# Order of the last stage: the turning of the second half's normed rows behind the first four experts of half 0, its gate behind the next four

## The reference

```python
scores = sigmoid(x @ gate.T)                      # 8 experts
sel    = top 2 of the better group of 4 (by scores + corr_bias)
top    = scores[sel] / (scores[sel].sum() + 1e-20)
lat    = x @ fc1.T                                # 256 -> 128
comb   = sum over sel of top[e] * relu2(lat @ w1[e].T) @ w2[e].T
out    = layernorm(x + comb @ fc2.T + relu2(x @ up.T) @ down.T)   # relu2(a) = max(a, 0)**2
```

## Time and profile before

| | |
|---|---|
| median of 3 runs | 1975.12 us (1972.39 to 1977.35) |
| the profiled execution's own time | 1973.6 us |
| its span, first to last instruction | 1971.5 us |
| TensorE busy | 94% of the span |
| VectorE, ScalarE, GpSimd busy | 69%, 44%, 44% |
| mean granted TensorE clock | 0.981 of full speed |

### The profile page before, as it was taken

One profiled execution on the slowest core, in us unless ns is written; L12 is line 12 of the kernel. 1 busy time (PEld: TensorE's weight loads), 2 busy tenths in 40 slices (PEclk: granted clock), 3 DMA queues, 4 the chain that ended last, 5 costly groups with the idle time before them and its releaser, 6 DMA issues.

```text
span 1971.5 us, 35531 instructions
## 1 busy us (share of the span) xinstructions
PE 1859.1 (94%) x11760; PEld 1623.9 (82%) x11760; DVE 1353.2 (69%) x3192; ACT 871.9 (44%) x1623; POOL 865.5 (44%) x1169
## 2 busy tenths in 40 slices
PE   7999999399999989999999999999999999999996
PEld 6888887289999977888788888878878878878885
DVE  5688888644444556786786886876876786786664
ACT  4445454333333424445445445445355445444443
POOL 4267777631111142454354354364265265255054
PEclk9999999599999989999999999999999999999998
DMA  4111222223332231211111221121112212111011
GB/s 155 65 65 64 75 96 87 87 75 99 107 103 86 96 106 44 66 44 60 64 51 47 50 79 44 44 87 44 44 67 65 43 47 85 38 49 54 12 44 65
DMA packets 81639, 133.04 MB, mean 67 GB/s; under 512 B 11328, under 2 KB 62144, under 8 KB 81376
## 3 DMA queue, kind: packets, MB, share of 16 engines
q1 hardware_dynamic: 71984, 104.96, 15.7%
q0 software_dynamic: 9520, 26.36, 5.5%
HBM read 105.57 MB, written 25.72 MB: 67 GB/s over the span
## 4 chain that ended last, share of the span: by engine, by line
PE 61%; DVE 7%; issue 5%; POOL 3%; ACT 3%; DMA 1%; POOLq 0%; DVEq 0%; ACTq 0%
PE c_ps L118 10%; PE c_ps L120 9%; PE c_ps L119 9%; PE b_ps L118 5%; PE b_ps L119 5%; PE b_ps L120 5%; PE c_ps L133 3%; PE c_ps L134 3%; PE c_ps L135 3%; PE c_ps L2023 2%; PE c_ps L2084 2%; PE c_ps L2086 2%; PE c_ps L2085 2%; POOL c_pool_tmp L97 1%; ACT b_win_raw L1610 1%
## 5 line engine op out<-in xcount | busy, mean ns | idle before, releaser
L1547 POOL TENSOR_TENSOR c_place<-c_shared_place,c_place 128x512 fp32r<-128x512 f32 x256 | 324.5, 1296 | 197.2 <-ACT c_place L1726 114.1
L1538 POOL DMA_INDIRECT c_gathered<-expert_results,c_slots x112 | 112.3, 1003 | 325.2 <-DVE c_pre L1778 301.7
L1937 DVE SCALAR_TENSOR_TENSOR c_shared_place<-c_ps,c_shared_place 128x512 f32<-128x512 f32 x256 | 170.4, 683 | 57.3 <-ACT c_shared_place L1718 57.1
L118 PE MATMUL c_ps<-c_place 128*128 128x256 f32 (+1 forms) x520 | 149.9, 288 | 10.4 <-DVE c_place L1850 6.4
L1726 ACT ACTIVATE c_place<-c_shared_place 128x512 fp32r<-128x512 f32 x128 | 80.3, 630 | 173.6 <-DVE c_shared_place L1937 172.6
L133 PE MATMUL c_ps<-c_downT_hi,c_place 128*128 128x256 f32 x512 | 151.4, 296 | 2.7 <-POOL c_place L1547 2.7
L119 PE MATMUL c_ps<-c_place 128*128 128x256 f32 (+1 forms) x520 | 147.9, 284 | 0.0
L120 PE MATMUL c_ps<-c_place 128*128 128x256 f32 (+1 forms) x520 | 147.8, 284 | 0.0
L134 PE MATMUL c_ps<-c_downT_lo,c_place 128*128 128x256 f32 x512 | 144.7, 283 | 0.0
L135 PE MATMUL c_ps<-c_downT_hi,c_place 128*128 128x256 f32 x512 | 144.6, 282 | 0.0
L1047 POOL DMA_INDIRECT b_xs<-x_rows,expert_tokens x56 | 57.9, 1033 | 196.5 <-PE b_ps L1228 176.4
(11 more groups left out here) (416 smaller groups left out, 6144.6 us busy)
## 6 DMA issues: line engine op xcount, KB each, us to landing
c_x2T<-score_rows SPq DMA_DIRECT2D x64, 512.0 KB, 5.5
b_win_raw<-xT SPq DMA_DIRECT2D x8, 1024.0 KB, 6.4
a_x_rows<-x SPq DMA_DIRECT2D x8, 1024.0 KB, 5.6
x_rows<-a_x SPq DMA_DIRECT2D x8, 1024.0 KB, 4.5
c_pre<-x_rows SPq DMA_DIRECT2D x8, 1024.0 KB, 5.5
out<-b_win_raw SPq DMA_DIRECT2D x16, 512.0 KB, 3.0
b_win_raw<-w_in SPq DMA_DIRECT2D x7, 1024.0 KB, 5.5
b_wout_raw<-w_out SPq DMA_DIRECT2D x7, 1024.0 KB, 6.3
```

The source lines that it names most:

```text
L118: pe.matmul(out, lh, rh, start=(j == 0), stop=False)
L1538: pool.indirect_dma_start(rows[:, a, :], None, d["ys"], bass.IndirectOffsetOnAxis(ap=slots[:, a, t:t + 1], axis=0), bounds_check=TRASH + P ...
L1547: pool.tensor_tensor(hid_lo[:, place, :], square[:, place % RING, :], f32(hid_hi[:, place, :]), ALU.subtract).then_inc(hid_split, 1)
L1937: v.scalar_tensor_tensor(square[:, place % RING, :], ps[:, s_bank(unit, k - lag), :], 0.0, factor, ALU.max, ALU.mult).then_inc(s_free, 1)
```

## The change

`ORDER` alone is changed, at four units: `expert (0, 0)` now stands ahead of `x3T 1`, `expert (0, 1)` ahead of `gate 1`, and `comb 0` ahead of `gateT 1`. All instructions stay the same. Since banks 4 and 5 are dealt out by the order, `comb 0` and `gateT 1` exchange theirs.

```diff
-             ("combine", 7), ("up", (0, 1)), ("ln2", 0), ("x3T", 1), ("expert", (0, 0)), ("gate", 1), ("expert", (0, 1)), ("gateT", 1),
-             ("comb", 0), ("up", (1, 0)), ("scoreT", 1), ("out", 0), ("latent", 1), ("up", (1, 1)), ("ln4", 0), ("expert", (1, 0)),
+             ("combine", 7), ("up", (0, 1)), ("ln2", 0), ("expert", (0, 0)), ("x3T", 1), ("expert", (0, 1)), ("gate", 1),
+             ("comb", 0), ("gateT", 1), ("up", (1, 0)), ("scoreT", 1), ("out", 0), ("latent", 1), ("up", (1, 1)), ("ln4", 0), ("expert", (1, 0)),
```

## The result

The changed kernel takes 1992.12 us (median of 4 runs, 1989.4 to 1995.15), the kernel before 1973.95 beside it (4 runs). The ratio is 1.009, with a 95% interval of 1.0077 to 1.0102: 18.2 us slower.

A forecast was written before the change was run, and what follows sets the result against it. TensorE, busy for 94% of the span, was taken to bound the kernel. New waits of 15.8 us plus 7.0 us for the clock made 22.8 us, from 1975.12 to 1997.9 us; range 1987 to 2006.

The forecast's parts named there:

- The part without the clock: Sum of TensorE's new waits over the eight batches: 7 x 1.91 + 2.41 = 15.8 us.
- Part 1: x3T 1 behind expert (0, 0): removing the 1.50 wait gains nothing, transposes cost +0.87, expert 4's wait of 0.33 goes.
- Part 2: gate 1 behind expert (0, 1): its six matmuls take 1.38 and comb 0 starts +0.03 us so far.
- Part 3: gateT 1 behind comb 0: VectorE's route chain follows comb's low part; scoreT is 1.91 us later, 1.54 a new wait.
- VectorE regains its distance in up (1, 1): Behind scoreT, VectorE and GpSimd regain their distance in up (1, 1), which TensorE paces; no size given.
- Part 4: TensorE's pause ahead of expert (0, 0) becomes 2.79 us and the clock falls in seven batches: 1.0 each, 7.0 us.
- The faster one: TensorE goes straight from up (0, 1) to expert (0, 0) while ScalarE norms; 10.3 us go: 1964.8, chance 0.05.

The follow-up runs named there:

- the pause filled: Changed kernel plus eleven matmuls of zeros where TensorE pauses ahead of expert (0, 0), in seven batches: 1988.31 us, ratio 1.0072.
- gateT inside and the pause filled: Changed kernel with gateT 1 issued behind comb 0's expert 3, banks exchanged, plus eleven matmuls of zeros ahead of expert (0, 0): 1982.2 us, ratio 1.0015.
- gateT alone: Kernel before with only gateT 1 moved behind comb 0; x3T 1 and gate 1 stay: 1985.29 us, ratio 1.0061.
- scoreT later: Changed kernel with latent 1 ahead of scoreT 1 instead of behind out 0: 1997.66 us, ratio 1.0125.
- gateT put back: Changed kernel with gateT 1 again ahead of comb 0, directly behind gate 1: 1989.12 us, ratio 1.0078.
- gateT inside comb: Changed kernel with gateT 1 issued on TensorE behind comb 0's expert 3, ahead of comb 0 on ScalarE and VectorE, banks exchanged: 1980.66 us, ratio 1.004.
- the splits first: Changed kernel with GpSimd's eight splits ahead of its scale chain, norm behind expert (0, 0), x3T 1 inside expert (0, 1), gateT 1 inside comb 0: 1952.07 us, ratio 0.9897.

## Why the prediction was right

**The sign and the size.** 1997.9 was forecast from 1975.12, +22.8; measured were +18.2. The range of 1987 to 2006 holds 1992.12. The part without the clock was forecast at 15.8 and measured at 15.4, with the pause filled; nearly all that is missing is in the clock. A batch with the clock up was forecast at 153.2 and took 153.05, with falls at 154.2 and took 153.81. The profiled execution's span grew by 21.6, of which 1.8 lie ahead of the first up.

**Part 1, x3T behind expert (0, 0).** Right. The wait for ScalarE went, and the expert met its own wait at the same 1437.86. The turning, uncovered, took 0.79 for the 0.87 forecast; the wait of 0.33 went. By itself, without route and clock, the part costs 0.31 a batch (0.37 forecast), as the run with gateT inside and the pause filled shows.

**Part 2.** Right: x3T's low part was done at 1466.23, which is 1454.12 with 12.11 taken off, near the 1454 forecast, and gate 1 had no wait.

**Part 3, the route chain.** Right, at 1.47 a batch for 1.54, shown by moving gateT alone. My 5.79 for the chain held to 0.23 (6.02), and scoreT came 1.59 behind its turn for the 1.54 forecast (1.37 of it as idle time in the trace). I also wrote that VectorE regains its distance in up (1, 1). In the changed kernel it does: behind scoreT no unit of half 1 waits. But the distance is small, and the run with scoreT later shows it: TensorE 1.37 sooner, and it waits 1.56 for VectorE at experts 0 and 4.

**Part 4, the clock.** The mechanism was right: the clock fell behind the long pause in all seven batches of the profiled execution. That it did so in every one was in part luck. With the same pause it fell in five of seven batches with gateT put back, in six with scoreT later and in three with gateT inside comb; what decides it no run here shows. The term of the sum that was mis-sized is the price of a fall: 0.76 a batch by the traces for the 1.0 taken, within the 0.6 to 1.4 given (0.61 in the fifth batch's timeline up to the end of expert (0, 0)). Two traces show it inside one execution. With gateT put back the two of the last six batches without a fall took 152.10 and 152.45 us, the three with a fall of 3.41 us 152.74 to 153.15. With gateT inside comb the three without took 151.48 to 151.75, the three with one 152.05 to 152.22. And it is no constant: with gateT alone a fall cost nothing, since waits stood behind it.

Seven times 0.76 is 5.3 us for the 7.0 of the sum. The medians give less, 18.2 - 15.4 = 2.7, but their intervals overlap. How many falls the executions behind a median hold can't be read from one profile: with gateT inside comb the four that weren't profiled had lower mean clocks than the profiled one, and took only 0.7 to 2.9 us more.

**The rivals.** The faster one, TensorE going straight on with the expert, needed the bank by 1435.1 and met it at 1437.7. It came true in the run with the splits first, in which ScalarE's norm and GpSimd's chain are moved too, and there it was worth more than its 10.3 us: 21.

## What to carry to other kernels

A wait at the head of a queue says who comes first, not who ends last: before moving work out from behind it, list the next waits behind it on that engine with the times at which they end, because what was hidden in them will have to be paid for at its new place. A long chain of small instructions belongs where its engine is idle and as early as its input allows; moved behind a unit of another engine, it delays everything in its own queue, and reordering the consumer doesn't bring that back. Joining short pauses into one long pause can cost the matmul clock as well.

## What the runs showed of the hardware

- In the changed kernel's profile a pause of TensorE of 2.76 to 2.87 us, with 0.6 more shortly behind it, was followed by 3.41 us at 1.2 GHz in seven batches of seven. The stretch began 0.5 to 2.2 us after the engine had resumed. The same pause in three other kernels (2.2 to 2.9 us) was followed by a fall in 14 batches of 21, four of them of 6.83 us, which began 0.7 to 0.8 us before the engine resumed. Pauses of 1.45 to 1.50, with the eight transposes behind them, were followed by none in the profile of before (seven batches) and by one in the run with gateT alone. Eleven matmuls of zeros in the long pause kept the clock at 1.00 in both runs that had them.
- The first instruction of the route chain (128x32) took 1.04 us beside a GpSimd split (before, at 1461.10) and 0.17 without one (changed kernel, at 1478.80); in the changed kernel two instructions of ln2 on 128x8 values still took 1.32 and 1.21 us beside the splits, where their like takes 0.17.
